# Two width tests instead of one, and a reordered opening, in a fused feed-forward and mixer kernel

## The chip, the cores and the metric

One core of a Trainium2 chip runs the whole program. The metric is the device time of one execution, in microseconds (us). Five engines work from queues of their own and meet at semaphores: TensorE (PE in the profile; PEld is its weight load), VectorE (DVE), ScalarE (ACT), GpSimd (POOL) and SyncE (SP), which here only issues transfers. Each engine runs its own list in order.

## The reference, cut to what matters

The input x has 8 x 1024 tokens of 256 values. Three stages follow each other; all is fp32.

```python
def ffn(x, ln_gamma, ln_beta, fc1_q, fc1_scales, fc1_bias, fc2_q, fc2_scales, fc2_bias):
    h = layernorm(x) * ln_gamma + ln_beta
    w1 = (fc1_q - 128) * fc1_scales      # 256 x 1024, scales per group of 128 rows
    y = silu(h @ w1 + fc1_bias)
    w2 = (fc2_q - 128) * fc2_scales      # 1024 x 256
    return x + 0.5 * (y @ w2 + fc2_bias)

x = x + 0.5 * ffn(layernorm(x))          # first feed-forward
x = x + mixer(layernorm(x))              # gates a, b, c, a scan over time, two projections
x = x + 0.5 * ffn(layernorm(x))          # second feed-forward
```

The weights fc1_q and fc2_q arrive as int32. The drawn values are 0 to 63, but any int32 is allowed.

## The kernel before, in words

The tokens are cut into NT = 16 tiles of TILE = 512 tokens. All of x stays on the chip (`resid`). A tile of a feed-forward goes through these steps. VectorE finds mean and variance (`statistics` L699, `variance` L708 to L721). GpSimd raises the variance to the power -1/2 and forms the shift (`rsqrt` L375 to L381). GpSimd and ScalarE or VectorE write the normalised tile `xhat` (`normalise`, L389, L559, L729), and GpSimd scales the residual (`residual` L400). TensorE transposes xhat, one transpose group for each of two halves c of the 256 channels (`turn` L1002). ScalarE rounds a half to the reduced type fp32r (`round_h` L551) and VectorE writes what the rounding lost (`lower_h` L745). So each product with the activations is made of two matmuls, one with the high and one with the low part.

The hidden layer of 1024 is taken in FC = 8 groups f. For each, TensorE multiplies the first 128 channels (`half_products`), ScalarE or VectorE scales the bank and adds the bias in place (`scale_half`, L576 and L739; groups 4 and 6 are VectorE's), TensorE adds the other 128 channels (`add_products`), ScalarE applies silu twice, once in full (L591) and once rounded (L593), and GpSimd subtracts the two (`g_low` L410). Then TensorE multiplies by the second layer (`fc2`, both matmul kinds at L1009), LAG = 4 groups behind, into three banks in turn, and VectorE adds each bank to `z_acc` (L762, `add_group`). An `fc2` that reuses a bank waits for VectorE's add of three fills earlier.

The order is written out by hand: each engine has a loop over tiles and, in it, over f, and tables (`TURN_AT`, `TURN_OUT_AT`, `H_LOWER_AT`, `RESIDUAL_AT`) say at which f the preparation of the next tile is put. `before` is 0 in the first tile of a stage, `behind` counts the tiles left. `ff0 == 0` marks the first feed-forward.

fp32r holds the weights minus 128 exactly as long as they are narrow. The kernel therefore looks for the largest absolute weight (`largest_of` L893, one reduction for each half of q1 and q2), joins the four maxima (L899), has TensorE turn them into a row (L1209), reduces the row and compares it with a limit (L905, L908). The flag decides a branch on TensorE: either the program with the high parts of the weights, or, for wide weights, the program with both parts. VectorE has a branch of its own on the same flag, in which it prepares the low parts (`prepare_wide`). With the drawn inputs the flag is 0 both times.

The opening before the first tile: 48 rows of small parameters are loaded, TensorE transposes them into columns (L994), and ScalarE copies these (L538). Then come ScalarE's half of the first normalise, the conversions of q1 and q2 from int32 (`convert_q1` L544, q2 at L645), and on GpSimd `prepare_columns` (L417 to L428). The contribution of ln_beta to the first layer's bias comes from 16 small matmuls (`beta_products` L1055), which VectorE folds into `bias` (`fold_beta`, L864 to L873). TensorE's list: transposes of the rows and of the first xhat, `beta_products(0)`, the transpose of the maxima, `beta_products(1)`, the branch, and the program.

## Time and profile before

| | before |
|---|---|
| median of 3 runs (lowest to highest) | 689.8 us (689.78 to 690.16) |
| the profiled execution | 690.4 us, of which span 687.6 us |
| TensorE busy | 668.0 us, 97% |
| ScalarE busy | 653.4 us, 95% |
| VectorE busy | 634.8 us, 92% |
| GpSimd busy | 604.8 us, 88% |

The span is the time from the first to the last recorded instruction; the rest lies around it. A busy share is an average over the three stages and the opening. Matmuls overlap each other, so a busy TensorE is not one at its peak. Times in the trace count from the start of the span. A row of the order of time gives start, length, engine, line, operation and the number of like instructions merged; behind it stands, in brackets, how long the engine was idle before and what ended that.

### The profile page before, as it was taken

The numbers are of one execution on the slowest core, as the hardware profiler recorded it, in microseconds if no ns is written. First come the engines' busy times: TensorE is split into PE (matmuls) and PEld (weight loads), VectorE is DVE, ScalarE is ACT, GpSimd is POOL, SyncE is SP. The second block draws the span as 40 slices with busy tenths as digits, with TensorE's granted clock in tenths as the row PEclk, the third lists the DMA queues.
The fourth block names the chain that finished last, engine by engine and source line by source line (L and its number), as shares of the span: only waits on it lengthen the run. The fifth ranks groups of instructions, "written<-read, shape, count | busy, mean of one in ns | idle before, by whom it ended". The sixth has DMA issues, their size and how long they took to land.

```text
span 687.6 us, 13669 instructions
## 1 busy us (share of the span) xinstructions
PE 668.0 (97%) x3224; PEld 539.2 (78%) x3224; DVE 634.8 (92%) x1329; ACT 653.4 (95%) x1095; POOL 604.8 (88%) x673
## 2 busy tenths in 40 slices
PE   3999999999999999999999999999999999999997
PEld 3678888888888878778877887788888888888885
DVE  5789999999999999889999998899999999999987
ACT  4899999999999999889999999999999999999994
POOL 4899999999999999857766789999999999999973
PEclk9999999999999999999999999999999999999999
DMA  8670000000000000000000000000000000000001
GB/s 254 172 236 4 1 0 0 0 0 0 0 0 0 1 0 2 1 1 1 0 0 0 0 1 1 30 33 32 31 31 31 31 31 31 31 31 32 32 32 63
DMA packets 19962, 20.22 MB, mean 29 GB/s; under 512 B 1564, under 2 KB 19666, under 8 KB 19922
## 3 DMA queue, kind: packets, MB, share of 16 engines
q1 hardware_dynamic: 19824, 19.74, 9.3%
q8 instruction: 16, 0.26, 0.2%
q14 instruction: 24, 0.20, 0.1%
q10 hardware_dynamic: 98, 0.02, 0.0%
HBM read 11.37 MB, written 8.39 MB: 29 GB/s over the span
## 4 chain that ended last, share of the span: by engine, by line
PE 90%; ACT 3%; DVE 3%; issue 2%; DMA 1%; ACTq 0%; POOL 0%; DVEq 0%; POOLq 0%
PE ps_z L1009 38%; PE ps_fc L1009 33%; PE ps_fc L1142 8%; PE ps_tr L1002 5%; PE ps_tr L1070 4%; PE ps_fc L1150 2%; PE ps_z L1002 1%; DMA rows<-in_L_attn_bc 1%; DVE z_acc L762 1%; ACT ps_fc L576 1%; ACT g_hi L593 1%; DVE stats L699 1%; ACT g_full L591 0%; DVE resid L887 0%; ACTq L530 0%
## 5 line engine op out<-in xcount | busy, mean ns | idle before, releaser
L410 POOL TENSOR_TENSOR g_lo<-g_full,g_hi 128x512 fp32r<-128x512 f32 x256 | 332.9, 1300 | 24.7 <-ACT g_hi L593 21.8
L762 DVE SCALAR_TENSOR_TENSOR z_acc<-ps_z,cols,z_acc 128x512 f32<-128x512 f32 (+1 forms) x449 | 322.2, 742 | 24.2 <-PE ps_z L1009 16.4
L1009 PE MATMUL ps_fc<-h_hi,q_sb 128*128 128x512 f32 x512 | 213.4, 417 | 1.4 <-ACT ps_fc L576 1.4
L1009 PE MATMUL ps_z<-g_hi,q_sb 128*128 128x512 f32 x512 | 202.4, 395 | 0.1
L1009 PE MATMUL ps_fc<-h_lo,q_sb 128*128 128x512 f32 x512 | 202.3, 395 | 0.0
L1009 PE MATMUL ps_z<-g_lo,q_sb 128*128 128x512 f32 x512 | 200.6, 392 | 0.0
L591 ACT ACTIVATE g_full<-ps_fc,safe_scale 128x512 f32<-128x512 f32 x256 | 194.8, 761 | 3.9 <-PE ps_fc L1009 2.2
L593 ACT ACTIVATE g_hi<-ps_fc,safe_scale 128x512 fp32r<-128x512 f32 x256 | 196.2, 766 | 0.0
L576 ACT ACTIVATE ps_fc<-ps_fc,bias,ratio 128x512 f32<-128x512 f32 x193 | 157.9, 819 | 1.8 <-DVE bias L873 1.8
L1009 PEld LDWEIGHTS ps_z<-g_hi,q_sb 128*128 128x128 f32 x512 | 96.1, 188 | 25.0 <-DVE z_acc L762 2.7
L1009 PEld LDWEIGHTS ps_fc<-h_hi,q_sb 128*128 128x128 f32 x512 | 97.3, 190 | 21.0 <-ACT ps_fc L576 2.1
L1009 PEld LDWEIGHTS ps_z<-g_lo,q_sb 128*128 128x128 f32 x512 | 96.1, 188 | 20.7
L1009 PEld LDWEIGHTS ps_fc<-h_lo,q_sb 128*128 128x128 f32 x512 | 97.6, 191 | 15.8
L375 POOL TENSOR_TENSOR rstd<-var_terms,minus_half 128x8 f32<-128x8 f32 (+1 forms) x48 | 70.7, 1472 | 11.7 <-DVE neg_mean L721 7.8
L400 POOL TENSOR_SCALAR resid<-resid,res_scale,shift 128x256 f32<-128x256 f32 x128 | 72.8, 570 | 0.2
L699 DVE BATCH_NORM_STATS2 stats<-resid 128x6 f32 (+1 forms) x192 | 69.2, 409 | 2.2 <-DMA resid<-in_L_attn_x 1.8
L583 ACT ACTIVATE z_acc<-ps_z,cols 128x512 f32<-128x512 f32 x64 | 58.0, 906 | 0.1
L389 POOL TENSOR_SCALAR xhat<-resid,rstd,shift 128x256 f32<-128x256 f32 x96 | 55.5, 579 | 0.2
L1142 PE MATMUL ps_fc<-wd_sb,q_int 128*128 128x256 f32 x240 | 54.6, 379 | 0.0
L739 DVE TENSOR_SCALAR ps_fc<-ps_fc,ratio,bias 128x512 f32<-128x512 f32 x63 | 50.9, 807 | 3.5 <-PE ps_fc L1009 3.5
L559 ACT ACTIVATE xhat<-resid,shift,rstd 128x256 f32 (+1 forms) x92 | 51.0, 602 | 0.0
L1002 PE MATMUL ps_tr<-ident,xhat 128*128 128x128 f32 x320 | 48.4, 274 | 2.1 <-ACT xhat L559 1.5
(110 smaller groups left out, 820.4 us busy)
## 6 DMA issues: line engine op xcount, KB each, us to landing
resid<-in_L_attn_x SPq DMA_DIRECT2D x15, 512.0 KB, 4.6
out_x<-resid SPq DMA_DIRECT2D x15, 512.0 KB, 2.9
q_int<-in_L_ffn_fc_q SPq DMA_DIRECT2D x4, 512.0 KB, 7.3
resid<-in_L_attn_x SPq DMA_DIRECT2D x2, 256.0 KB, 3.0
out_x<-resid SPq DMA_DIRECT2D x2, 256.0 KB, 2.7
wd_sb<-in_L_attn_Wd SPq DMA_DIRECT2D x1, 256.0 KB
wy_raw<-in_L_attn_Wy SPq DMA_DIRECT2D x2, 64.0 KB
bias_rows<-in_L_attn_by SPq DMA_DIRECT2D x1, 128.0 KB
```

The lines of the kernel that those rows point to most:

```text
L375: nc.gpsimd.tensor_tensor(rstd[:, 0:n, :], var_terms[:, par, 0:n, :], minus_half[:, 0:n, :], ALU.pow).then_inc(rstd_ready, 1)
L400: last = nc.gpsimd.tensor_scalar(resid[:, t, a, :], resid[:, t, a, :], res_scale[:, a:a + 1], shift[:, 1, a:a + 1], ALU.mult, ALU.add)
L410: nc.gpsimd.tensor_tensor(g_lo[:, g % 4, :], g_full[:, g % 4, :], g_hi[:, g % 4, :].bitcast(F32), ALU.subtract).then_inc(g_ready, 1)
L576: nc.scalar.activation(bank, bank, ACT.Identity, bias=bias[:, f:f + 1], scale=ratio[:, f:f + 1]).then_inc(scaled_on_act, 1)
L583: nc.scalar.activation(z_acc[:, par, n, :], bank_of(0, n, par), ACT.Identity, bias=col(R_B2 + n), scale=col(R_S2 + n)).then_inc(z_begun[n], 1)
L591: nc.scalar.activation(g_full[:, g % 4, :], bank, ACT.Silu, scale=scale)
L593: nc.scalar.activation(g_hi[:, g % 4, :], bank, ACT.Silu, scale=scale).then_inc(g_hi_ready, 1)
L699: last = nc.vector.bn_stats(stats[:, a, :], resid[:, t, a, :])
L762: nc.vector.scalar_tensor_tensor(out=z, in0=bank_of(g, n, par)[:, tokens], scalar=col(R_S2 + KC * g + n), in1=z, op0=ALU.mult, op1=ALU.add ...
L1002: last = nc.tensor.transpose(bank[:, a * P:(a + 1) * P], xhat[:, par, a, c * P:(c + 1) * P], ident[:, :])
L1009: last = nc.tensor.matmul(out, w, v, start=start and i == 0, stop=stop and i == len(pairs) - 1, skip_group_check=not start)
L1142: nc.tensor.matmul(mix_bank(t, par, half)[:, a * D:(a + 1) * D], xn[:, par, k, at:at + P], wd_sb[:, k, :], start=False, stop=False, skip_g ...
```

## The change

TensorE's first four half products and three added products of the first tile (`opening`) are taken out of the program and stand behind a test of q1's width alone. A second test, of q1 and q2, stands behind them and ahead of the rest. VectorE's reductions of q2, the second join and the second flag move behind the first flag and the bias, with the statistics of tile 1 between them. Its half of the normalise of tile 1 moves from f = 3 of the first tile to behind the second branch. In the first tile, GpSimd's `rsqrt` for tile 1 goes from f = 0 to f = 1, behind the first `g_low`, and its normalise to f = 2. The transposes, roundings and lowerings for tile 1 go from f = 3 and 5 (lowerings 4 and 6) to f = 6 and 7. The small parameters are transposed into a bank of `ps_fc1`, and the first xhat no longer waits for their copy. ScalarE normalises first, then converts, copies the columns, converts again and rounds. Half of q2 is converted on GpSimd. GpSimd also clears `q1_low` at the start.

```diff
+        FIRST_TURN_AT, FIRST_LOWER_AT = (6, 7), (6, 7)
+        FIRST_RESIDUAL_AT = {4: (0, 1), 5: (2, 3)}
+        def first_or(ff0, before, first, usual):
+            return first if ff0 == 0 and not before else usual[before]
 # gpsimd
+            nc.gpsimd.memset(q1_low[:, :, :].bitcast(F32), 0.0).then_inc(q1_low_zero, 1)
...
-                        elif ff0 == 0:
+                        if ff0 == 0 and not before and f == 1:
                             rsqrt(ln0 + 1, 1, True)
-                        if ff0 == 0 and not before and f == 1:
+                        if ff0 == 0 and not before and f == 2:
                             normalise(ln0 + 1, 1, 1, halves[0], True)
...
                     prepare_columns()
+                    pool.wait_ge(q2_loaded[0], 16)
+                    nc.gpsimd.tensor_scalar(q2_sb[:, q2_halves[0], :], q2_int[:, q2_halves[0], :], -ZERO_POINT, None,
+                                            ALU.add).then_inc(q2_ready[0], 1)
                     residual(ln0, 0, 1)
 # scalar
-            act.wait_ge(rows_turned, 1)
-            nc.scalar.activation(cols[:, :], ps_tr2[:, 0:ROWS], ACT.Copy).then_inc(cols_ready, 1)
-            act.wait_ge(cols_ready, 1)
...
                     normalise(ln0, 0, 0, halves[1], xhat_half_ready)
                     convert_q1(0)
+                    act.wait_ge(rows_turned, 1)
+                    nc.scalar.activation(cols[:, :], ps_fc1[:, 3, 0:ROWS], ACT.Copy).then_inc(cols_ready, 1)
+                    act.wait_ge(cols_ready, 1)
+                    convert_q1(1)
                     for c in range(KC):
                         round_h(ln0, ff0, 0, c, bank=(ps_tr, ps_tr2)[c])
-                    convert_q1(1)
-                    for k in range(KC):
-                        act.wait_ge(q2_loaded[k], 16)
-                    nc.scalar.activation(q2_sb[:, :, :], q2_int[:, :, :], ACT.Copy,
-                                         bias=-ZERO_POINT).then_inc(q2_ready, 1)
+                    act.wait_ge(q2_loaded[1], 16)
+                    nc.scalar.activation(q2_sb[:, q2_halves[1], :], q2_int[:, q2_halves[1], :], ACT.Copy,
+                                         bias=-ZERO_POINT).then_inc(q2_ready[1], 1)
 # vector, in the first tile
-                            if ff0 == 0:
-                                normalise(ln0 + 1, 1, 1, halves[1])
 # vector, ahead of the tiles
-                    for k, part in enumerate(q2_halves):
-                        largest_of(KC + k, q2_int[:, part, :].rearrange("p g d -> p (g d)"), q2_loaded[k])
-                    join_largest()
+                    join_largest(0, KC)
                     dve.wait_ge(scale_done, 3)
                     nc.vector.reciprocal(inverse[:, :], safe_scale[:, :]).then_inc(ratio_ready, 1)
-                    lower_h(ln0, ff0, 0, 0)
-                    find_width()
+                    find_width(0, KC + 2)
                     dve.wait_ge(ratio_ready, 1)
                     nc.vector.tensor_tensor(ratio[:, :], cols[:, R_S1:R_S1 + FC], inverse[:, :], ALU.mult)
+                    for c in range(KC):
+                        lower_h(ln0, ff0, 0, c, (ps_tr, ps_tr2)[c])
+                    dve.wait_ge(beta_done, KC)
+                    fold_beta(1)
+                    prepare_wide_q1()
+                    largest_of(KC, q2_int[:, q2_halves[0], :].rearrange("p g d -> p (g d)"), q2_loaded[0])
                     dve.wait_ge(x_loaded[1], 16)
                     statistics(1)
                     variance(ln0 + 1, 1)
-                    dve.wait_ge(beta_done, KC)
-                    fold_beta(1)
-                    lower_h(ln0, ff0, 0, 1, ps_tr2)
-                    prepare_wide()
+                    largest_of(KC + 1, q2_int[:, q2_halves[1], :].rearrange("p g d -> p (g d)"), q2_loaded[1])
+                    join_largest(1, 2 * KC + 2)
+                    find_width(1, 2 * KC + 4)
+                    prepare_wide_q2()
+                    normalise(ln0 + 1, 1, 1, halves[1])
+            def prepare_wide_q2():
+                dve.wait_ge(flag_ready, 2)
+                wide = dve.value_load(wide_flag[0:1, 1:2], min_val=0, max_val=1)
+                with dve.If(wide > 0):
...
 # tensor
-                    for f in range(FC):
+                    for f in range(0 if before or ff0 else LAG, FC):
...
+            def opening():
+                for f in range(LAG):
+                    half_products(0, 0, f, 0)
+                    if f >= 1:
+                        add_products(0, 0, f - 1, 0)
+            def turn_largest(turn):
+                nc.tensor.transpose(ps_z[0:1, 0, 0:P], largest[:, 4 + turn:5 + turn],
+                                    ident[:, :]).then_inc(largest_turned, 1)
-            pe.wait_ge(cols_ready, 1)
...
-            pe.wait_ge(largest_found, 5)
-            nc.tensor.transpose(ps_z[0:1, 0, 0:P], largest[:, 4:5], ident[:, :]).then_inc(largest_turned, 1)
+            pe.wait_ge(largest_found, KC + 1)
+            turn_largest(0)
             pe.wait_ge(q1_ready, KC)
             beta_products(1, q1_sb).then_inc(beta_done, 1)
             pe.wait_ge(flag_ready, 1)
+            q1_wide = pe.value_load(wide_flag[0:1, 0:1], min_val=0, max_val=1)
+            with pe.If(q1_wide < 1):
+                q1_parts = (q1_sb,)
+                opening()
+            with pe.Else():
...
+            pe.wait_ge(largest_found, 2 * KC + 3)
+            turn_largest(1)
+            pe.wait_ge(flag_ready, 2)
+            wide = pe.value_load(wide_flag[0:1, 1:2], min_val=0, max_val=1)
             with pe.If(wide < 1):
                 q1_parts, q2_parts = (q1_sb,), (q2_sb,)
                 program()
```

## Rows read from the trace of the kernel before

**Rows 1.** The page's slices of granted clock; then windows: PE, PEld, DVE, ACT, POOL, clock.
```profile
PEclk9999999999999999999999999999999999999999
...
100.00:150.00 50.00, 50.00 (x245) 41.17 (x244) 48.33 (x98) 49.83 (x84) 48.36 (x55) 1.00 0.00 0
```

**Rows 2.** Order of time of TensorE, from the first transpose to 38 us.
```profile
9.72 0.31 PE L994 MATMUL ps_z<-ident,rows 48*128 48x48 f32 x1 [9.72 <-DMA rows<-in_L_attn_bc]
11.55 1.09 PE L1002 MATMUL ps_tr<-ident,xhat 128*128 128x128 f32 x4 [1.52 <-ACT xhat L559]
...
14.85 0.37 PE L1209 MATMUL ps_z<-ident,largest 128*1 128x128 f32 x1
...
16.94 0.77 PE L1009 MATMUL ps_fc<-h_hi,q_sb 128*128 128x512 f32 x1
...
19.64 0.76 PE L1009 MATMUL ps_fc<-h_hi,q_sb 128*128 128x512 f32 x1 [0.64 <-ACT ps_fc L576]
...
23.61 0.63 PE L1009 MATMUL ps_fc<-h_lo,q_sb 128*128 128x512 f32 x1
24.85 0.63 PE L1002 MATMUL ps_tr<-ident,xhat 128*128 128x128 f32 x4 [0.61 <-issue]
...
28.07 0.39 PE L1009 MATMUL ps_fc<-h_hi,q_sb 128*128 128x512 f32 x1
...
36.88 0.50 PE L1009 MATMUL ps_z<-g_hi,q_sb 128*128 128x512 f32 x1
...
37.94 0.50 PE L1009 MATMUL ps_z<-g_hi,q_sb 128*128 128x512 f32 x1
```

**Rows 3.** Order of time of VectorE, 10 to 40 us.
```profile
10.57 1.22 DVE L893 TENSOR_REDUCE largest<-q_int 128x1 f32<-128x1024 int32 x1 [0.29 <-DMA q_int<-in_L_ffn_fc_q]
...
15.57 0.14 DVE L908 TENSOR_SCALAR wide_flag<-largest 1x1 int32<-1x1 f32 x1
...
17.78 0.25 DVE L864 TENSOR_TENSOR beta_terms<-ps_z,cols 128x16 f32<-128x16 f32 x2
...
18.48 0.17 DVE L873 TENSOR_TENSOR bias<-bias,inverse 128x8 f32<-128x8 f32 x1
...
19.72 1.41 DVE L699 BATCH_NORM_STATS2 stats<-resid 128x6 f32<-128x256 f32 x4 [0.41 <-issue]
...
21.80 0.73 DVE L729 TENSOR_SCALAR xhat<-resid,rstd,shift 128x256 f32<-128x256 f32 x2
25.98 0.82 DVE L739 TENSOR_SCALAR ps_fc<-ps_fc,ratio,bias 128x512 f32<-128x512 f32 x1 [3.46 <-PE ps_fc L1009]
...
29.19 0.75 DVE L762 SCALAR_TENSOR_TENSOR z_acc<-ps_z,cols,z_acc 128x512 f32<-128x512 f32 x1 [0.16 <-PE ps_z L1009]
...
36.09 3.38 DVE L762 SCALAR_TENSOR_TENSOR z_acc<-ps_z,cols,z_acc 128x512 f32<-128x512 f32 x5
```

**Rows 4.** Order of time of GpSimd, from the start to 38 us.
```profile
1.82 0.52 POOL L367 MEMSET bias_raw<- 128x512 f32 x1
5.96 1.66 POOL L375 TENSOR_TENSOR rstd<-var_terms,minus_half 128x8 f32<-128x8 f32 x1 [3.62 <-DVE neg_mean L721]
...
7.88 0.20 POOL L381 TENSOR_TENSOR shift<-rstd,neg_mean 128x8 f32<-128x8 f32 x1
...
17.95 1.67 POOL L375 TENSOR_TENSOR rstd<-var_terms,minus_half 128x8 f32<-128x8 f32 x1 [4.19 <-DVE neg_mean L721]
...
22.21 1.47 POOL L410 TENSOR_TENSOR g_lo<-g_full,g_hi 128x512 fp32r<-128x512 f32 x1 [2.14 <-ACT g_hi L593]
...
36.59 1.30 POOL L410 TENSOR_TENSOR g_lo<-g_full,g_hi 128x512 fp32r<-128x512 f32 x1
```

**Rows 5.** Order of time of ScalarE: the first scalings with the bias.
```profile
18.74 1.42 ACT L576 ACTIVATE ps_fc<-ps_fc,bias,ratio 128x512 f32<-128x512 f32 x2 [1.78 <-DVE bias L873]
```

**Rows 6.** Windows, 30 to 35 us (columns as in Rows 1).
```profile
30.00:35.00 5.00, 5.00 (x23) 3.69 (x22) 5.00 (x10) 5.00 (x10) 4.63 (x6) 1.00 0.82 251
```

**Rows 7.** The page's DMA issues: KB each, us from issue to landing.
```profile
out_x<-resid SPq DMA_DIRECT2D x2, 256.0 KB, 2.7
```

More of the change, by code:

```diff
@@ L169, in macaron_kernel @@
         q1_ready = sem("q1_ready")
-        q2_ready = sem("q2_ready")
+        q2_ready = [sem(f"q2_ready{k}") for k in range(KC)]
         beta_ready = sem("beta_ready")
@@ L1097, in tile @@
                             y_products(NT - 1, 1)
-                        if (behind or ff0 == 0) and f in TURN_AT[before]:
-                            c = TURN_AT[before].index(f)
+                        turn_at = first_or(ff0, before, FIRST_TURN_AT, TURN_AT)
+                        if (behind or ff0 == 0) and f in turn_at:
+                            c = turn_at.index(f)
                             if c and before:
@@ L1212, in _ @@
             pe.wait_ge(flag_ready, 1)
-            wide = pe.value_load(wide_flag[0:1, 0:1], min_val=0, max_val=1)
+            q1_wide = pe.value_load(wide_flag[0:1, 0:1], min_val=0, max_val=1)
[3 more added lines that the diff above has]
+            with pe.Else():
+                q1_parts = (q1_sb, q1_low)
+                pe.wait_ge(q1_low_ready, KC)
+                pe.wait_ge(bias_ready, 1)
+                for k in range(KC):
+                    last = beta_products(k, q1_low)
+                last.then_inc(beta_low_done, 1)
+                pe.wait_ge(wide_bias_ready, 1)
+                opening()
+            pe.wait_ge(largest_found, 2 * KC + 3)
+            turn_largest(1)
+            pe.wait_ge(flag_ready, 2)
+            wide = pe.value_load(wide_flag[0:1, 1:2], min_val=0, max_val=1)
             with pe.If(wide < 1):
@@ L1218, in _ @@
                 q1_parts, q2_parts = (q1_sb, q1_low), (q2_sb, q2_low)
-                pe.wait_ge(wide_ready, KC + 1)
-                pe.wait_ge(bias_ready, 1)
-                for k in range(KC):
-                    last = beta_products(k, q1_low)
-                last.then_inc(beta_low_done, 1)
-                pe.wait_ge(wide_bias_ready, 1)
+                pe.wait_ge(q2_low_ready, 1)
                 program()
```

67 lines of the change are left out of this document (37 added, 30 removed).

## Prediction

> **What bounds the kernel now.** I read the page's clock and the windows first [rows 1]: between 100 and 150 us TensorE is busy all of the 50 us, at a granted clock of 1.00. TensorE sets the pace there, ScalarE (49.83) is close behind, and neither is touched by the change. The change lives in the first 40 us. A delay or a gain counts only if it is still there when TensorE becomes dense for good. Then I read TensorE's order of time [rows 2]. It idles 1.52 us until 11.55 for ScalarE's half of the first normalised tile. Its first wide product is at 16.94. The next product group waits for the bias and starts at 19.64. The last product of the opening groups is at 23.61; a transpose follows at 24.85 after 0.61 idle. The last waits of the start are at 36.88, which starts 0.04 after VectorE's first add of a run ends (36.09 + 0.75 = 36.84), and at 37.94, which starts 0.05 after GpSimd's subtraction ends (36.59 + 1.30 = 37.89) [rows 2 to 4]. So the kernel's end hangs on three times near 37 us: TensorE's own work, VectorE's run of adds from 36.09 [rows 3], and GpSimd's.
>
> **The change, part by part.** Times are those of the profiled execution: span 687.6 us, 690.4 us measured, against a median of 689.8. I sum a difference and apply it to the median.
>
> *Start of the opening groups.* The transposes no longer wait for the copy of the columns. The shift is ready at 7.88 + 0.20 = 8.08 [rows 4]. ScalarE's two blocks, which before lay between 10.03 and 11.5 (so under 1.5 us), are done by 9.6 at the latest. The transposes follow the transpose of the rows: 9.72 + 0.31 = 10.03. From first transpose to first wide product before: 16.94 - 11.55 = 5.39. After: 15.4. The first flag moves with it: 15.57 + 0.14 - 1.5 = 14.2, so 1.2 us ahead of its use, as before (16.94 - 15.71 = 1.23). The two reductions of q1 (about 1.22 each, the second ending before 10.57 [rows 3]) are early enough.
>
> *Bias.* VectorE lowers both halves of h (0.75 each, as every 512-wide pass of it) until 15.6, then folds the bias: 17.78 to 18.48 + 0.17 is 0.87, so the bias is ready at 16.5 against 18.65. ScalarE scales 0.09 behind it before [rows 5]; now the first product itself (16.6) is about as late, and the scaling starts at 16.65 against 18.74. The group at 19.64 moves by the same 2.09, to 17.55, and the end of the opening groups from 23.61 + 0.43 = 24.04 to 21.95.
>
> *The second test, a new wait.* It follows the opening groups on TensorE, and all of TensorE's later work is queued behind it. VectorE must have the maximum of q2. After the bias (16.5) comes the first branch. What a branch costs: VectorE before shows 0.41 of idle behind it, but its sequencer could have begun as early as 18.48, giving 19.72 - 18.48 = 1.24 [rows 3]; on TensorE 1.23 were enough. Bounds 0.41 and 1.24. I take 1.0, because little stands ahead of either branch now that could hide it. Then: first q2 maximum 17.4 to 18.6 (1.22), statistics and variance of tile 1 to 20.7 (19.72 to 21.80 is 2.08), second maximum to 21.9, join to 22.1. TensorE's transpose, scan and flag take 14.85 to 15.71, 0.86: from 22.15 to 23.0. Plus 1.0 for the branch: TensorE resumes at 24.0, after 2 us of idle, against 25.24 before (24.85 and some 0.4 for its transposes), with that transpose group of 0.4 still owed. Of the 2.09 gained some 0.85 are left here.
>
> The Trainium skill, "Advanced Engine Details and Errata", section Control Flow Timing, gives about 0.11 us for a compare-and-branch. By that price alone (the loading of the register not in it) the sum below would be at its lower end, 689.8; rows 3 show at least 0.41 exposed.
>
> *VectorE behind the branch.* Its normalise of tile 1 is now behind the second flag: 24.0 (the shift is ready at 23.7, see GpSimd). Then 0.7 for it, 2.08 for the statistics and variance of tile 2, and only then the scaling for group 4: 26.75 to 27.55. Before it stood idle 3.46 us ahead of that scaling [rows 3], and TensorE did not wait. Now TensorE, which would get to the group's second half at 26.8 (twelve matmuls of 0.23), waits to 27.65, against 28.07 before. From there to VectorE's add of group 1 before: 29.19 - 28.07 = 1.12; after: 28.77. From that add to the one at 36.09 VectorE ran 6.90 without a gap (5.00 of 5 us busy from 30 to 35) [rows 6]. After, both lowerings of h for tile 1 lie in it, where before one stood ahead of the add at 29.19: 6.90 + 0.7 = 7.6, and 28.77 + 7.6 = 36.4. That is 0.3 later than 36.09, and TensorE's wait at 36.88 becomes one until 37.2.
>
> *GpSimd.* The power for tile 1 stood in idle time (17.95, after 4.19 idle [rows 4]): 1.67 and two operations of 0.20, 2.07 in all. It now stands behind the first subtraction, in the busy run. That run starts 2.09 earlier (20.1 against 22.21) and is 2.07 longer: the subtraction at 36.59 stays within 0.05. The shift is ready at 20.1 + 1.5 + 2.1 = 23.7. So GpSimd alone gives the gain back too. Clearing q1_low (2048 elements) is added at 2.3 us; 512 took 0.52, so about 2.1, in 3.62 of idle. Were that cover gone it would cost up to 2. Converting half of q2 there: subtraction and xhat rows bound it by 1.3 to 4 us (128x256 takes about 0.55, so 1024 some 2.2); it runs from 11.6, the residual blocks behind it (2.2) end by 18 even at the upper bound, ahead of 20.1. Without cover it would be 2 us on the power. ScalarE's shorter conversion of q2 is hidden before and after.
>
> *Sum.* +0.3 us at 37 us, where VectorE is last; dense from there. With the branch at 0.41: the q2 chain 0.6 shorter, the flag bound by TensorE's 21.95, the normalise by the shift at 23.7: 0.0. With 1.24, twice 0.24 more: +0.8. Forecast 689.8 + 0.3 = 690.1, own range 689.7 to 690.7.
>
> **Rivals.**
>
> *A, the clock, slower.* The granted clock reads 1.00 in every slice [rows 1], but the matmuls' own times tell the two levels: 0.63 each and (23.61 - 19.64) / 9 = 0.44 apart until 23.61 (1.2 GHz), 0.39 each and half as far apart at 28.07 (2.4 GHz) [rows 2]. The rise came between 24.04 and 24.85, after dense work since 19.64 and a wait of 0.64 before that. Now the dense stretch is 17.55 to 21.95 and then TensorE stands for 2 us. If it has not risen by then, the first groups of the program run at 0.43: eight matmuls from 24.0 to 27.4, a rise near 27.8, the half at 28.5 instead of 27.65, VectorE's add at 29.7 instead of 28.77. +0.9 on the sum: +1.2, 691.0. It decides when the rise comes after 25. For it: the idle stretch. Against it: 4.4 us of dense work, as long as the 4.4 to 5.2 that sufficed before.
>
> The Trainium skill, "TensorE: Matmul & The Clock Gate", Part 1, says that sustained activity releases the clock, that an idle stretch takes it back, and that the moment varies from run to run with the phase of a free-running monitor; by that rule rival A would come in some executions and not in others, at the time just given.
>
> *B, the branch stalls on instructions, slower.* TensorE's queue is empty at the second branch; if the instructions behind it must be fetched, VectorE and TensorE resume later. No row shows it; the nearest transfer is 2.7 us from issue to landing [rows 7]. 24.0 becomes 25.7, and the sum +0.3 + 1.7 = +2.0: 691.8. It decides if the resumption is later than 23.0 + 1.3. Against it: the branch before cost at most 1.23.
>
> The Trainium skill, "Runtime: NRT & Kernel Launch", Instruction fetch mechanics, says that a taken branch outside the loaded blocks must fetch first; the If here falls through into its program, so the rule need not bite.
>
> *C, faster.* VectorE and GpSimd recover more than I think, and TensorE keeps its own lead: 1.25 at the resumption, less 0.4 for the owed transpose, plus some 0.3 lost in the two waits at 36.88 and 37.94: -1.2, 688.6. It needs VectorE's 7.6 us to shrink. Against it: from 30 to 35 VectorE is busy 5.00 us and GpSimd 4.63 [rows 6].
>
> *D, it does nothing measurable of what it says:* the opening starts at 16.9 because the columns stay the last input. Then the flag chain and GpSimd's run both slip by up to 1.5: 691.5. The rows give the order 8.08 before 9.72, so 3%.
>
> **How the numbers follow.** Forecast 0.60, A 0.17, B 0.07, C 0.13, D 0.03. A change under 0.2% (1.4 us) can't be told from none here: 688.4 to 691.2 is the same. Faster needs C and a little more: 0.06. Slower needs B, D or the worse half of A with a slow branch: 0.12. The range takes in the greater part of A and C: 688.8 to 691.3.
>
> **What would show it.** Right: first wide product near 15.4, second group near 17.55, one idle stretch of TensorE of 1.5 to 2.3 us before 24, a wait for VectorE's scaling near 27.6, the run of adds at 36.4, GpSimd's subtraction for group 6 within 0.3 of 36.59, and nothing different behind 40 us but a constant shift. Wrong: matmuls 0.43 apart behind 24 us (A), resumption after 25 (B), VectorE idle between 29 and 36 (C).

## The result, and the profile after

The changed kernel took 692.22 us (median of 6 runs, 691.61 to 693.74) against 689.79 for the kernel before beside it (6 runs, 689.05 to 690.51): ratio 1.0043, interval 1.0033 to 1.0053, which is 2.3 to 3.7 us. By the medians it is 2.4 us slower, where 0.3 was forecast, and outside the range. Two executions among the experiments (969.01 us in experiment 6, 2394.3 in experiment 7) lie far off all others and are left out of every ratio.

The profiled execution has a span of 689.8 us (691.7 measured), 2.2 more than before. One difference between the two profiled executions has nothing to do with the code: the rows landed at 8.79 us here and at 9.72 in the one of before [rows 2]; over all profiles of this study they landed between 8.21 and 9.72. The early times below are about 0.9 smaller for that reason alone.

The span and the time around it have to be kept apart, since the change moved both:

| kernel (executions) | median time | median span (lowest to highest) | outside the span |
|---|---|---|---|
| before (68, beside the experiments) | 689.4 to 689.9 | 687.2 (686.4 to 688.3) | 2.2 to 2.8 |
| changed (6) | 692.22 | 690.4 (689.8 to 691.9) | 1.8 to 1.9 |
| experiment 1 (5) | 693.56 | 690.3 (690.2 to 691.2) | 2.1 to 3.6 |
| experiment 3 (11) | 690.16 | 688.0 (686.6 to 688.6) | 2.1 to 2.8 |
| experiment 6 (5) | 692.23 | 690.0 (689.0 to 690.7) | 1.8 to 3.3 |
| experiment 10 (11) | 690.08 | 688.2 (687.7 to 689.6) | 1.8 to 1.9 |
| experiment 11 (11) | 688.71 | 686.0 (685.7 to 687.1) | 2.1 to 2.8 |
| experiment 12, last (11) | 688.29 | 685.8 (685.4 to 686.2) | 2.2 to 2.8 |

So the program itself lost some 3.2 us, and 0.7 of it does not show in the time because less lies outside the span. Why less lies there is not shown.

Next, where the loss is. TensorE's first transposes of a finished tile's sum (called the tile's mark below; one comes every 16.4 us) start at 43.54 before and 45.94 after, those of the next tile at 59.97 and 62.40, of the fifth at 109.26 and 111.75, and those near 440 us at 440.10 and 442.62. The loss is complete at 46 us, and what follows is shifted by nearly a constant. Counted from the landing of the rows, the first mark stands at 33.82 before and 37.15 after, 3.3 later. In the windows, TensorE is less busy than before between 24 and 38.6 us and as dense as before between 100 and 150 [rows 1]. The columns are those of rows 1, then DMA share and GB/s; the first line is of the kernel before, the others of the changed one.

```profile
24.00:38.60 14.60, 13.91 (x62) 10.35 (x62) 11.60 (x26) 14.52 (x25) 14.23 (x19) 1.00 0.78 222
```

```profile
24.00:38.60 14.60, 13.51 (x54) 9.90 (x54) 13.43 (x36) 11.68 (x19) 12.91 (x18) 0.90 0.74 222
100.00:150.00 50.00, 50.00 (x247) 41.29 (x246) 48.33 (x99) 49.82 (x83) 48.25 (x58) 1.00 0.00 0
```

TensorE in order of time answers to [rows 2]:

```profile
8.79 0.31 PE L1019 MATMUL ps_fc<-ident,rows 48*128 48x48 f32 x1 [8.79 <-DMA rows<-in_L_attn_bc]
9.27 1.10 PE L1027 MATMUL ps_tr<-ident,xhat 128*128 128x128 f32 x4 [0.17 <-POOL xhat L400]
...
14.61 0.77 PE L1034 MATMUL ps_fc<-h_hi,q_sb 128*128 128x512 f32 x1 [0.16 <-issue]
...
16.79 0.76 PE L1034 MATMUL ps_fc<-h_hi,q_sb 128*128 128x512 f32 x1
...
20.43 0.40 PE L1034 MATMUL ps_fc<-h_lo,q_sb 128*128 128x512 f32 x1
22.18 0.27 PE L1236 MATMUL ps_z<-ident,largest 128*1 128x128 f32 x1 [1.35 <-DVE largest L915]
23.78 0.79 PE L1034 MATMUL ps_fc<-h_hi,q_sb 128*128 128x512 f32 x1 [1.33 <-DVE wide_flag L924]
...
28.34 0.50 PE L1034 MATMUL ps_fc<-h_hi,q_sb 128*128 128x512 f32 x1
...
34.47 0.63 PE L1027 MATMUL ps_tr<-ident,xhat 128*128 128x128 f32 x4 [0.67 <-DVE h_lo L758]
...
39.42 0.50 PE L1034 MATMUL ps_z<-g_hi,q_sb 128*128 128x512 f32 x1 [1.09 <-DVE z_acc L775]
```

The reader is to see that the opening did move: its wide products start at 14.61 and end at 20.43 + 0.40 = 20.83, against 16.94 and 23.61 + 0.63 = 24.24. Then the waits: 1.35 and 1.33 around the second test, 0.67 for a lowering of h, and at the end the wait for VectorE's run of adds, which ends at 39.42 instead of 36.88.

VectorE in order of time answers to [rows 3]:

```profile
15.46 0.34 DVE L889 TENSOR_TENSOR bias<-bias,inverse 128x8 f32<-128x8 f32 x1
...
16.62 1.22 DVE L909 TENSOR_REDUCE largest<-q_int 128x1 f32<-128x1024 int32 x1 [0.82 <-issue]
17.75 1.40 DVE L712 BATCH_NORM_STATS2 stats<-resid 128x6 f32<-128x256 f32 x4
...
19.60 1.07 DVE L728 TENSOR_SCALAR var_terms<-mean_var 128x4 f32<-128x4 f32 x1
20.58 0.16 DVE L730 TENSOR_SCALAR var_terms<-mean_var 128x4 f32<-128x4 f32 x1
...
22.80 0.14 DVE L924 TENSOR_SCALAR wide_flag<-largest 1x1 int32<-1x1 f32 x1
24.25 1.25 DVE L742 TENSOR_SCALAR xhat<-resid,rstd,shift 128x256 f32<-128x256 f32 x2 [1.30 <-issue]
25.42 1.39 DVE L712 BATCH_NORM_STATS2 stats<-resid 128x6 f32<-128x256 f32 x4
...
27.47 0.81 DVE L752 TENSOR_SCALAR ps_fc<-ps_fc,ratio,bias 128x512 f32<-128x512 f32 x1
...
29.58 0.75 DVE L775 SCALAR_TENSOR_TENSOR z_acc<-ps_z,cols,z_acc 128x512 f32<-128x512 f32 x1 [0.59 <-PE ps_z L1034]
...
36.95 0.43 DVE L728 TENSOR_SCALAR var_terms<-mean_var 128x4 f32<-128x4 f32 x1
37.29 1.35 DVE L730 TENSOR_SCALAR var_terms<-mean_var 128x4 f32<-128x4 f32 x1
38.55 0.16 DVE L734 TENSOR_SCALAR neg_mean<-mean_var 128x4 f32<-128x4 f32 x1
38.63 3.37 DVE L775 SCALAR_TENSOR_TENSOR z_acc<-ps_z,cols,z_acc 128x512 f32<-128x512 f32 x5
```

The same pass over 4 elements takes 0.16 us at 20.58 and 1.35 at 37.29. GpSimd's rows say why:

```profile
19.36 1.28 POOL L421 TENSOR_TENSOR g_lo<-g_full,g_hi 128x512 fp32r<-128x512 f32 x1 [3.04 <-ACT g_hi L603]
20.89 1.67 POOL L386 TENSOR_TENSOR rstd<-var_terms,minus_half 128x8 f32<-128x8 f32 x1 [0.25 <-DVE neg_mean L734]
...
24.22 1.13 POOL L400 TENSOR_SCALAR xhat<-resid,rstd,shift 128x256 f32<-128x256 f32 x2
...
37.31 1.30 POOL L421 TENSOR_TENSOR g_lo<-g_full,g_hi 128x512 fp32r<-128x512 f32 x1
```

The two longest passes over 4 elements end with a GpSimd operation: 19.60 + 1.07 = 20.67 with 19.36 + 1.28 = 20.64, and 37.29 + 1.35 = 38.64 with 37.31 + 1.30 = 38.61. The normalise at 24.25 (1.25 us; 0.73 before) lies beside GpSimd's blocks of 24.22, and each of its two blocks ends 0.15 behind one of GpSimd's (24.92 and 25.50, 24.77 and 25.35). Reductions, statistics and passes that read PSUM are never long. A wait of this kind is counted as busy time, so it shows in the duration of a row and nowhere in a bracket.

The Trainium skill, "SBUF — State Buffer", Who interferes with whom, says that a VectorE pass in a two-port mode and a GpSimd operation take a shared pair of ports as an exclusive lock, each for its whole instruction; that tensor_scalar can be in such a mode, except in the form that also writes its accumulator; and that reductions on trn2 never are. This trace agrees (1.07, 1.35 and 1.25 us against 0.16 and 0.73), and the accumulator form is what the experiments use below.

### The profile page after: what moved, and what is told of

The parts are those of the page before. It is cut to its first block, busy times and chain, and to the rows that moved or that the text cites. A ratio compares the mean times of both kernels' runs of the same rounds, so it can differ in the third digit from the quotient of the medians.

```text
span 689.8 us, 13684 instructions
## 1 busy us (share of the span) xinstructions
PE 668.9 (97%) x3225; PEld 540.4 (78%) x3225; DVE 638.0 (92%) x1332; ACT 653.0 (95%) x1095; POOL 609.9 (88%) x675
## 4 chain that ended last, share of the span: by engine, by line
PE 89%; DVE 4%; ACT 3%; issue 2%; POOL 1%; DMA 0%; DVEq 0%; ACTq 0%
PE ps_z L1034 37%; PE ps_fc L1034 32%; PE ps_fc L1168 8%; PE ps_tr L1027 5%; PE ps_tr L1095 4%; PE ps_fc L1176 2%; DVE stats L712 1%; PE ps_z L1027 1%; ACT g_hi L603 1%; ACT ps_fc L586 1%; DVE z_acc L775 1%; DMA resid<-in_L_attn_x 0%; DVE h_lo L758 0%; ACT g_full L601 0%; ACT h_hi L561 0%
```

## The experiments

The theory after the result, V: VectorE's serial run from the bias to 38.63 sets the loss, lengthened by passes that wait for GpSimd (called L, the lock, where it is tested alone). Its rivals: T, the second test itself; K, the clock, which fell (the products of 23.78 to 26.5 are 0.43 apart, those behind 26.89 are 0.23 apart); the new places of the transposes in the first tile; and later P, where tensors stand in memory. Each was timed beside the kernel before, whose medians were 689.4 to 689.9.

**1. Take the second test out.** On VectorE and TensorE of the changed kernel:

```diff
-                    largest_of(KC, q2_int[:, q2_halves[0], :] ..., q2_loaded[0])
...
-                    largest_of(KC + 1, q2_int[:, q2_halves[1], :] ..., q2_loaded[1])
-                    join_largest(1, 2 * KC + 2)
-                    find_width(1, 2 * KC + 4)
-                    prepare_wide_q2()
...
-            turn_largest(1)
-            pe.wait_ge(flag_ready, 2)
...
+            q1_parts, q2_parts = (q1_sb,), (q2_sb,)
+            program()
```

This leaves the treatment of wide second-layer weights out. 

> The changed kernel without its second test: no maxima of q2, no second flag, no second branch; the rest of the program follows the opening groups directly (q2 is taken to be narrow, as it is here). Theory V (VectorE's serial run through the first tile sets the time, and its one-source passes wait for GpSimd's operation to end): the flag chain goes, but VectorE's normalise still waits for GpSimd's shift, which is behind the first subtraction, so it starts near 23.0 instead of 24.25; the run of adds moves by that: about -1.2 us against the changed kernel, 691.0, still over the kernel before. Rival T (the second test and TensorE's 2.9 us idle around it are the whole loss): all of it comes back, 689.8 or less. Rival K (the clock that falls in the idle stretch): TensorE stays at 2.4 GHz, about -1.5.

Measured: 693.56 (1.0049, interval 1.0035 to 1.0064). Nothing is gained, where V itself expected 691.0. The 1.3 us more than in the changed kernel lie outside the span; in the span the two are equal (690.3 and 690.4). Of this kernel, in order of time, VectorE and TensorE:

```profile
22.82 1.68 DVE L742 TENSOR_SCALAR xhat<-resid,rstd,shift 128x256 f32<-128x256 f32 x2 [3.97 <-POOL shift L392]
...
26.54 1.24 DVE L734 TENSOR_SCALAR neg_mean<-mean_var 128x4 f32<-128x4 f32 x1
```

```profile
28.55 0.80 PE L1029 MATMUL ps_fc<-h_hi,q_sb 128*128 128x512 f32 x1 [3.74 <-DVE ps_fc L752]
```

TensorE now idles 3.74 us in one piece for VectorE's scaling, which stands at 27.69, where it stood (27.47) with the test. So T falls as the sole cause: without the test, VectorE waits for GpSimd's shift, then pays 0.95 and 1.08 for the lock. But this kernel does not test V alone. Behind the idle 3.74 us the clock fell here too: TensorE's products are 0.43 apart from 28.55 to 33.84, VectorE stands idle 1.52 us for one of them (until 30.67), and its run of adds starts at 39.27 although the variance ahead of it hardly waited (0.32, 0.16 and 0.16 us). In place of the test stands, in part, the clock.

**2. Filler on TensorE, to hold its clock.** Unread products around the second transpose of maxima:

```diff
+            for _ in range(4):
+                nc.tensor.matmul(ps_z[:, 1, :], q1_sb[:, 0, 0:P], h_hi[:, 0, 0, :], start=True, stop=True)
             turn_largest(1)
+            for _ in range(5):
+                nc.tensor.matmul(ps_z[:, 1, :], q1_sb[:, 0, 0:P], h_hi[:, 0, 0, :], start=True, stop=True)
```

> The changed kernel with nine matmuls of 512 columns, whose result nobody reads, in TensorE's idle stretch (four ahead of the transpose of the second maxima, five behind it), to hold the clock. Theory V: TensorE resumes near 23.9 at 2.4 GHz, but then waits longer for VectorE's scaling of group 4 near 27.5: within 0.3 of the changed kernel. Rival K: the 3 us of slow matmuls behind the idle stretch were the loss: -1.0 to -1.5, about 691.0.

Measured: 692.52 (1.0044, 1.003 to 1.0058). TensorE in order of time:

```profile
23.78 0.49 PE L1034 MATMUL ps_fc<-h_hi,q_sb 128*128 128x512 f32 x1 [0.17 <-issue]
...
29.22 0.50 PE L1034 MATMUL ps_fc<-h_hi,q_sb 128*128 128x512 f32 x1 [2.45 <-DVE ps_fc L752]
```

The clock stayed up, and TensorE came sooner to a longer wait (2.45). That wait is longer for two reasons: TensorE was early, and the scaling stood at 28.35 instead of 27.47, since with the faster products GpSimd's subtraction of 27.00 lay on the variance of tile 2 (1.04 us at 27.25, where the changed kernel had 0.17). So K happens, and taking it away gains nothing in the end; what the slow products would cost without the lock is not separated.

**3. Only the new places of the transposes and lowerings,** in the kernel before, on TensorE, ScalarE and VectorE:

```diff
+        FIRST_AT = (6, 7)
...
-                        if (behind or ff0 == 0) and f in TURN_AT[before]:
+                        turn_at = first_or(ff0, before, TURN_AT)
+                        if (behind or ff0 == 0) and f in turn_at:
```

> The kernel before, with one part of the change alone: the transposes, roundings and lowerings for tile 1 at f = 6 and 7 of the first tile instead of 3 and 5 (lowerings 4 and 6). No second test, no reordered opening. Theory V: both lowerings (0.66 each) now lie in VectorE's run ahead of its adds, and the second transpose must wait for the first lowering, since they share a bank: 0.7 to 1.2 us slower than before, 690.5 to 691.0, or 1.3 more where the variance of tile 3 then meets a subtraction. Rival T: no change against before, as the loss is in the second test.

Measured: 690.16 (11 runs; 1.0008, 0.9999 to 1.0017), where V expected 0.7 to 1.2 more than before: a miss by the time (0.4), though 0.7 in the span (688.0 against 687.3). The interval reaches from no change to 1.2 us, so this is a part of the loss at most, and not clear of none.

**4. The order on VectorE.** Statistics and variance of tile 2 go behind the scaling that TensorE waits for:

```diff
-                        if not before and f == 3:
+                        if not before and f == (3 if ff0 else 4):
```

> The changed kernel with the statistics and the variance of tile 2 put behind VectorE's scaling of group 4 in its list, no longer ahead of it. Theory V1 (TensorE's early wait for that scaling is what costs): the scaling at 25.5 instead of 27.5, -1 us or more, 691.2. Theory V2 (VectorE is full from its normalise at 24.3 to the run of adds, so its sum counts and not the order): gains only its idle 0.8 at most, 691.4 to 692.2.

Measured: 691.88 (1.0038, 1.0023 to 1.0052). The scaling came 2.0 sooner (25.45), yet the run of adds started at 39.16, behind a variance pass of 1.35 at 37.82. That fits the expectation that VectorE's sum decides and not its order, but the clock is a rival that this run leaves standing: behind an idle stretch like the changed kernel's, TensorE's products are 0.43 apart from 23.93 to 29.13, 5.2 us instead of 3.1, and VectorE idles for them:

```profile
29.33 0.75 DVE L775 SCALAR_TENSOR_TENSOR z_acc<-ps_z,cols,z_acc 128x512 f32<-128x512 f32 x1 [1.01 <-PE ps_z L1034]
```

The six executions of this kernel have spans from 689.4 us, at a mean granted clock of 0.999, to 692.2, at 0.992. In the changed kernel (0.993 to 0.998) and in experiment 10 (0.995 to 1.000) time and clock do not go together so.

**5. The variance's small passes on GpSimd,** for tiles 1 and 3:

```diff
+                if type(ln) is int and ln in (1, 3):
...
+                    nc.gpsimd.tensor_scalar(var_terms[:, par, 0, :], mean_var[:, :, 1], 1.0 + EPS, EPS * EPS,
+                                            ALU.mult, ALU.add).then_inc(terms_made, 1)
```

> The changed kernel with the three small passes behind the variance (two variance terms and the negated mean) of tiles 1 and 3 on GpSimd instead of VectorE: the same work, where no operation of GpSimd can hold it up. Theory V: VectorE loses the waits of 0.9 us (tile 1, in the flag's path) and of some 1.4 us (tile 3, ahead of the run of adds at 38.63); GpSimd's run gets some 0.5 us longer twice. Run of adds near 37.0, time -1.0 to -2.0: 690.3 to 691.3. Rival (the waits are accidental and hidden, the loss is in the second test or in the clock): within 0.3 of the changed kernel, or 0.5 slower for GpSimd's added work.

Measured: 695.74 (1.0084, 1.0069 to 1.0099), a miss. The shift came 0.9 later (23.66), the normalise took 1.68 in the lock and the variance of tile 2, left on VectorE, 1.23; TensorE idled 3.76 for the scaling. Some 2 us more were lost between the first tile and the next: 1.52 there are a wait at 67.36 for VectorE's residual blocks, behind a variance pass that waited 1.84 (64.81). The granted clock was 0.993 in the three slowest of its five executions and 0.997 and 0.995 in the others, so not all of its loss need be the passes. The passes gained on neither engine in a form that needs the lock.

**6. The power for tile 1 ahead of the first subtraction,** on top of experiment 1:

```diff
-                        if ff0 == 0 and not before and f == 1:
+                        if ff0 == 0 and not before and f == 0:
                             rsqrt(ln0 + 1, 1, True)
```

> The kernel without the second test, with GpSimd's power for tile 1 back ahead of its first subtraction (f = 0 instead of 1). The statistics of tile 1 are done at 18.9, so the shift is ready near 21.0 instead of 22.8. Theory V (VectorE's list normalise, statistics 2, variance 2, scaling of group 4 starts at the shift and holds TensorE): the scaling comes near 25.9 instead of 27.7, TensorE's wait of 3.7 us shrinks by 1.8, time -1.5 to -2 against the kernel without the second test: 691.5 to 692. Rival (GpSimd's subtractions bound the first tile): the first subtraction is 1.6 later, so no gain or a loss.

Measured: 692.35 (692.23 without the one execution that is far off; 1.0042, 1.0029 to 1.0056). By the time that is 1.2 to 1.3 better than experiment 1, where 1.5 to 2 were expected, but nearly all of it lies outside the span: in the span it is 0.3 (690.0 against 690.3), a miss. VectorE of this kernel:

```profile
21.35 2.64 DVE L742 TENSOR_SCALAR xhat<-resid,rstd,shift 128x256 f32<-128x256 f32 x2 [2.24 <-POOL shift L392]
...
26.13 1.30 DVE L730 TENSOR_SCALAR var_terms<-mean_var 128x4 f32<-128x4 f32 x1
```

The normalise starts 1.5 sooner than in experiment 1 and takes 1.0 longer, and the variance of tile 2 then waits as well, so the scaling stands at 27.44 for 27.69. The lock takes back most of what the better order gave; the clock fell here too (products 0.43 apart from 28.30 to 31.74).

**7. The same passes in a form that writes the accumulator,** in variance and normalise. The values that this kernel writes are wrong, those of experiment 8, whose second scalars are 0, are right. So in that form the second scalar seems not to be added, which would leave the small constant out of the variance terms and the shift out of VectorE's half of the normalised block; this was not tested by itself. The unread sums take 32 bytes a partition, behind `res_scale`.

```diff
-                                            ALU.mult, ALU.add)
+                                            ALU.mult, ALU.add, accum_out=unread[:, 0:1])
```

> The changed kernel with every one-source pass of VectorE between two places in SBUF in the normalisation (the variance terms, the negated mean, VectorE's blocks of the normalise) written with a second output, a sum that nobody reads; same inputs, same main output, same order. Theory L (these passes wait for a running operation of GpSimd because of the way they use the memory's ports, and the form with a sum does not): no such pass ends together with a GpSimd operation any more, the passes of 4 elements take 0.2 us, the run of adds comes 1 to 2 us earlier, time 690.5 to 691.3. Rival: the coincidences are accidental, or any pass waits: the same long passes, within 0.3 of the changed kernel.

Measured: 695.05 (1.0082, 1.0068 to 1.0095), a miss by the time. The trace says two things. The lock was gone: passes of 0.15 and 0.16, a normalise of two times 0.54, and the run of adds at

```profile
35.79 3.38 DVE L777 SCALAR_TENSOR_TENSOR z_acc<-ps_z,cols,z_acc 128x512 f32<-128x512 f32 x5
```

2.84 earlier than 38.63. But the six tiles from the fifth mark to the eleventh took 99.85 us instead of 98.57: a new loss outside the change.

**8. The form only where its values are right,** the variance of tiles 1 to 3, second scalar 0 (the small constant folded into the first), with a tensor of 16 bytes a partition for the unread sums, declared behind res_scale. 

> The changed kernel with the three small passes of the variance of tiles 1, 2 and 3 (of the first feed-forward alone) in the form with a sum that nobody reads; it takes one scalar, so EPS is folded into the factor, which changes the result by some 1e-6. VectorE's normalise keeps its form. Theory L: in this form the passes do not wait for GpSimd; the run of adds of the changed kernel (38.63) comes 1.5 to 2.3 us earlier, as it did by 2.8 where the normalise had that form as well, and all of it is kept: time 690.0 to 690.9. Rival (VectorE's total is not what sets the first tile, or the waits only move on to the next pass): within 0.4 of the changed kernel.

Measured: 696.05 (1.0099, 1.0085 to 1.0112), a miss by the time. The run of adds started at 36.31, the first mark came at 43.84 (45.94), and then the same six tiles took 99.88.

**9. The 16 bytes alone,** in the kernel before, read and written by nothing:

```diff
         res_scale = sb("res_scale", [P, SUB])
+        pad = sb("pad", [P, 4])
```

> The kernel before with 16 unused bytes in each partition behind the tensor res_scale, and nothing else. Theory P (the place of the tensors behind it sets how far TensorE's matmuls of 512 columns are apart): 0.2335 instead of 0.2275 us apart, 5 us slower, about 695. Rival (the place is harmless; the free form or its extra reads slow the rest): 689.7 as before.

Measured: 694.94 (1.0082, 1.0068 to 1.0096). Its windows, to be held against [rows 1]:

```profile
100.00:150.00 50.00, 50.00 (x242) 40.73 (x241) 47.48 (x97) 49.10 (x82) 47.95 (x55) 1.00 0.00 0
```

TensorE is busy throughout at the same granted clock and does 242 products where it did 245 (247 in the changed kernel, so the count alone says little). The six tiles from the fifth mark to the eleventh, 109.08 to 208.97, took 99.89 us against 98.52. P is shown: where the later tensors stand is worth 5 us. All of it is lost in the two feed-forwards: from the last mark of the first to the first of the second, with the mixer between them, pass 163.24 us against 163.25. It explains experiments 7 and 8, and nothing of the change, whose dense part runs as before (98.57).

**10. Experiment 8 with the 16 bytes behind all other tensors.** This is the test of the whole account: V without its variance waits should come out at the forecast.

```diff
         wc_raw = sb("wc_raw", [P, KC, N])
+        unread = sb("unread", [P, 4])
...
+                    nc.vector.tensor_scalar(var_terms[:, par, 0, :], mean_var[:, :, 1], 1.0 + EPS, 0.0,
+                                            ALU.mult, ALU.add, accum_out=unread[:, 0:1])
+                    nc.vector.tensor_scalar(var_terms[:, par, 1, :], mean_var[:, :, 1], 4.0 * (1.0 + EPS), 0.0,
+                                            ALU.mult, ALU.add, accum_out=unread[:, 1:2])
```

> The changed kernel with the free form of the variance of tiles 1 to 3, with its unread sum at the end of the list of tensors, so that no other tensor moves. Theory L with P (the free form saves what the trace of the first tile showed, 2.1 us at 44 us; what was lost later, 1.3 us in every 100, came from the place of the tensors, which 16 added bytes had moved): spacing of TensorE as in the changed kernel, 2.1 us faster than it, 690.1. Rival (the form itself slows the rest): 695 to 696 again.

Measured: 690.08 (11 runs; 1.0007, 0.9998 to 1.0016). VectorE of this kernel:

```profile
19.64 0.16 DVE L727 TENSOR_SCALAR_CACHE_REDUCE var_terms<-mean_var 128x4 f32<-128x4 f32 x1
...
23.01 1.47 DVE L751 TENSOR_SCALAR xhat<-resid,rstd,shift 128x256 f32<-128x256 f32 x2 [0.91 <-POOL shift L393]
...
26.47 0.82 DVE L761 TENSOR_SCALAR ps_fc<-ps_fc,ratio,bias 128x512 f32<-128x512 f32 x1
...
36.03 0.15 DVE L729 TENSOR_SCALAR_CACHE_REDUCE var_terms<-mean_var 128x4 f32<-128x4 f32 x1
36.18 4.26 DVE L784 SCALAR_TENSOR_TENSOR z_acc<-ps_z,cols,z_acc 128x512 f32<-128x512 f32 x6
```

With both tests and every move of the change in place, three kinds of 4-element pass in another form give back 2.1 us: of 2.4 by the time, of 3.2 in the span, where 1.0 is left (688.2 against 687.2). The normalise still pays 0.74 to the lock; no run has a form of it with both scalars and without the wait.

**11. What each half of the change is worth.** The kernel before with its one test, and only the reordered opening:

```diff
-            act.wait_ge(rows_turned, 1)
-            nc.scalar.activation(cols[:, :], ps_tr2[:, 0:ROWS], ACT.Copy).then_inc(cols_ready, 1)
...
+            nc.scalar.activation(cols[:, :], ps_fc1[:, 3, 0:ROWS], ACT.Copy).then_inc(cols_ready, 1)
...
+                    lower_h(ln0, ff0, 0, 1, ps_tr2)
+                    dve.wait_ge(beta_done, KC)
+                    fold_beta(1)
```

> The kernel before, with its single test of all weights, and of the change only the reordered opening: ScalarE normalises before it copies the columns, the columns go through another bank, the transposes do not wait for them, and VectorE folds the bias ahead of the statistics of tile 1. Turns and lowerings for tile 1, VectorE's normalise, GpSimd's order and the conversions stay as before. Theory V: opening groups near 15.5 instead of 16.9, the bias 2 us earlier, VectorE keeps its slack ahead of the scaling of group 4 and GpSimd its power in idle time, so 1 to 1.5 us are kept: 688.3 to 688.8, faster than both. Rival (something that hangs on the data's arrival bounds the first tile, so that nothing of an earlier opening is kept): 689.8.

Measured: 688.71 (11 runs; 0.9986, 0.9977 to 0.9995). The reordering is a gain of 1.0 us, in the time as in the span; what stands behind the second test, and what it pushes together, costs 3.5 (4.4 in the span). What came earlier is the bias, ready at 17.05 instead of 18.65; the wide products start at 16.46 for the 15.5 expected, since the single test still needs the maxima of q2.

**12. On top of experiment 11.** The accumulator form in it, with the 16 bytes behind res_scale, once with the transposes at their old places and once, as the last line has it, at f = 4 and 6:

```diff
         res_scale = sb("res_scale", [P, SUB])
+        unread = sb("unread", [P, 4])
...
+                    nc.vector.tensor_scalar(var_terms[:, par, 0, :], mean_var[:, :, 1], 1.0 + EPS, 0.0,
+                                            ALU.mult, ALU.add, accum_out=unread[:, 0:1])
...
+        FIRST_TURN_AT, FIRST_LOWER_AT = (4, 6), (5, 7)
```

> The kernel with the reordered opening and one test, with the same free form of the variance of tiles 1 to 3. Theory L: there the passes waited 0.5 (tile 2, ahead of the normalise that TensorE's turn waits for) and 0.3 (tile 3): 0.3 to 0.7 faster than with the reordered opening alone: 688.0 to 688.4. Rival: no change, 688.7.

> That kernel with the transposes for tile 1 at f = 4 and 6 (instead of 3 and 5) and their lowerings at 5 and 7 (instead of 4 and 6) in the first tile, so that TensorE, which there idled 1.35 us ahead of the first of them, goes on with group 4. Theory V: TensorE's wait goes, but a lowering moves into VectorE's run ahead of the adds (0.66), so of 1.3 some 0.3 to 0.7 are kept: 687.5 to 688.1. Rival (GpSimd's run of subtractions bounds the first tile): no gain.

Measured: 694.02 (1.0067) and 693.95 (1.0066), two misses: both carry P's price (242 products in the window of 50 us), and the places make no difference beside it. With the 16 bytes at the end and the old places:

> The kernel with the reordered opening, one test and the free form, its unread sum at the end of the list. L with P: 0.2 to 0.7 faster than the reordered opening alone (688.7): 688.0 to 688.5. Rival: 694 again.

Measured: 688.88 (0.9987, 0.9977 to 0.9996), a miss: no gain over 688.71 (in the span 686.2 against 686.0). So the form by itself gains nothing there. Its variance is done at 21.35 and its normalise takes 0.82, but TensorE waits 1.40 for it, for its transposes stand too early. Last, both together:

```diff
         wc_raw = sb("wc_raw", [P, KC, N])
+        unread = sb("unread", [P, 4])
...
+        FIRST_TURN_AT, FIRST_LOWER_AT = (4, 6), (5, 7)
```

> The kernel with the reordered opening, the free form and the transposes for tile 1 at f = 4 and 6 (lowerings at 5 and 7), the unread sum at the end of the list. Theory V: the first turn_back near 42.6 (43.87 with the moved tensors, 43.42 with the earlier transposes), 0 to 0.5 slower than with the transposes at 3 and 5, since a lowering has moved into VectorE's run: 688.2 to 688.9. Rival: TensorE's idle time was the bound and 0.5 to 1 is gained: 687.5.

Measured: 688.29 (11 runs, 687.92 to 688.64; 0.9978, 0.9969 to 0.9987). The time lies in V's range, but V had expected it 0 to 0.5 slower than with the earlier places, and it is 0.6 faster (0.4 in the span): the rival, that TensorE's idle time there was the bound, has the direction right. It beats both kernels: 1.6 us under the one before, 3.9 under the changed one. Its rows landed at 9.72 as in the profile of before, so the two compare directly: TensorE's first mark stands at 41.83 against 43.54, VectorE's run of adds at 34.51 against 36.09.

## Why the prediction was wrong, step by step

*The step that failed* is the price of VectorE's passes in "the second test, a new wait" and "VectorE behind the branch": the statistics and variance taken at 2.08, the normalise at 0.7, and the run of adds at 6.90 + 0.7. I took these durations from the trace of before and moved the instructions to other neighbours. Three of them met a GpSimd operation there:

- Statistics and variance of tile 1, in front of the flag: from 17.75 to 20.73, 2.98 for 2.08: +0.9.
- Normalise: 24.25 to 25.42, 1.17 for 0.7: +0.5.
- Variance of tile 3, ahead of the run of adds: from 36.95 to 38.63, 1.68, where before it lay between 35.58 and 36.09, 0.51: +1.17. With the second lowering (0.68) and an idle 0.22 behind ScalarE's rounding, 6.90 becomes 8.97 (38.63 - 29.58 = 9.05 measured) for my 7.6.

The sum closes. I forecast the run of adds at 36.4, 26.7 behind the landing of the rows; it came at 38.63 - 8.79 = 29.8, 3.2 later. The three passes are 2.6 of it and the idle 0.22 another part; the rest is spread over small terms. With my 0.3 that makes 3.5, against 3.3 at the first mark and 3.2 in the span. That the time shows only 2.4 of it is the 0.7 outside the span, a term my sum did not have: I applied a difference of spans to a median of times.

Experiment 10 takes the first and the third away and is left with 690.08; the sum said 690.1. That closeness is luck in good part: the normalise's wait is still in it, and in the span this kernel is 1.0 over the one before and not 0.3.

*Most of my other terms held.* First transpose to first wide product: 14.61 - 9.27 = 5.34 for 5.39. The branch on VectorE behind the bias: an idle 0.82 for 1.0, behind a last bias row of 0.34 us for 0.17 (a pass with two sources, which ends with a residual block of GpSimd at 15.79), 1.16 in all for 1.17. Variance to flag: 2.2 for 2.3. Flag to TensorE's first product: 23.78 - 22.94 = 0.84 for 1.0. On VectorE the second branch was dearer: flag to normalise 1.31 for 1.0. Statistics and variance of tile 2, which met no GpSimd operation: 2.05 for 2.08. TensorE's wait for the scaling of group 4 came, at 28.34 for 27.65. GpSimd's subtraction stood at 37.31 for 36.59, 0.7 later, more than the 0.3 I allowed. Both are 0.9 later still when counted from the landing of the rows. The subtraction's part in the loss was the load that it put on VectorE; TensorE did not wait for it. The wait at 34.47 was not in the sum: the second transpose of tile 1 writes the bank that the first lowering still reads.

*Rival A* happened in the trace: the products at 23.78 to 26.5 are 0.43 apart and 0.63 long, the slow level, after 2.9 us in which TensorE did one small transpose; they are 0.23 apart from 26.89 on. But its price of 0.9 did not come on top, for VectorE was later still, and with the clock held up the time was no better (experiment 2). In experiments 1 and 4, where the slow stretch lasted longer, VectorE did wait for TensorE. *B* did not: 0.84 is under 1.3. *C* needed VectorE's 7.6 to shrink, and it grew. *D* did not: the opening moved. No rival of mine had VectorE's own passes getting longer. The bounds of my sum should have allowed for it, for the kernel before shows it. Its groups by line on VectorE (busy time, mean ns of one, idle before), with the same operation on the same shape 32 times in each:

```profile
L715 DVE TENSOR_SCALAR var_terms<-mean_var 128x4 f32<-128x4 f32 x32 | 13.4, 420 | 2.0
L717 DVE TENSOR_SCALAR var_terms<-mean_var 128x4 f32<-128x4 f32 x32 | 5.2, 164 | 0.0
```

A mean of 420 ns beside one of 164 for equal work is the lock, already there: of the 128 passes of 4 elements behind the variances of that trace, 37 take over 0.26 us, and each of the 37 starts while a GpSimd operation runs. It was the unknown cost, three times on the path, and had to stand in the range.

What stays open: the change loses 3.5 us against its own reordering, and the waits for GpSimd account for 2.1 by experiment 10. The remaining 1.4 (690.08 against 688.71; 2.2 in the span) must lie in what experiment 10 keeps: the second test's stop of TensorE, the clock that falls in it, the normalise behind it and the late transposes. It was not split further. Nor is it shown why the changed kernel has less time outside its span.

## What to carry to other kernels

Don't move an instruction at its old duration: look at the spread of the same form over the trace first, and where equal passes differ in their mean or a tiny one is at times many times its median, look at what the neighbouring engine ran when it ended. A wait between two engines that share a resource shows as busy time, not as idle. Compare spans as well as times, for a change can move the part outside. And give a new tensor, however small, its place behind all others until the dense part of the trace is seen to be unchanged.

## What the runs showed of the hardware

- A one-source VectorE pass from SBUF to SBUF waits for a running GpSimd operation, however small: 0.16 us became 1.07 and 1.35 for 4 elements (1.84 at 64.81 in experiment 5), two blocks of 256 (0.73) became 1.25 to 2.64. The form with an accumulator output took 0.15 to 0.16 at all its places, with a read of the accumulator of 0.08 beside it, and 0.54 for each block of 256, also beside GpSimd operations. A two-source pass of 8 elements took 0.34 for 0.17 beside a residual block of GpSimd, but 0.17 beside its power operation (18.48 in the kernel before).
- Sixteen bytes a partition ahead of later tensors made TensorE's dense part 1.4% slower from mark to mark (99.89 against 98.52), at a granted clock of 1.00, and the kernel 5 us. In the mixer nothing was lost (163.24 and 163.25 us between the feed-forwards' marks). Which tensor's place it is was not tried.
- After 2.9 us nearly without work TensorE was back at 1.2 GHz for 3.1 us (23.78 to 26.89), then at 2.4 GHz again. Behind much the same gap (20.75 to 23.93) it stayed there for 5.2 us in experiment 4. With the filler it did not fall.
